# The response of the second half through the columns of U, in stacked bands

## What is computed

```python
U_o = gram_schmidt(U); V_o = gram_schmidt(V)        # 256 x 32 each
basis = U_o @ V_o.T
pooled = hidden.mean(axis=1)
h1 = relu(pooled @ gate_w1.T + gate_b1)
base_act = sigmoid(h1 @ gate_w2.T + gate_b2)
strength = base_act * sigmoid(score)
feats = (hidden @ basis) @ basis.T[:, :32]
response = feats @ resp_w.T + resp_b + safety_bias
out = hidden + strength * response
```

## Time and profile before

| | us |
|---|---|
| median of 3 runs | 1368.19 |
| lowest and highest | 1367.77, 1368.98 |
| profiled execution, its own time | 1369.96 |
| span of the profiled execution | 1367.8 |
| first half, about | 0 to 880 |
| turn between the halves, about | 880 to 905 |
| second half, about | 905 to 1368 |

### The profile page before, as it was taken

The page is one execution under the profiler, slowest core; times in us unless marked ns, Lnnn a source line. Parts: engine busy times, 40 slices in busy tenths (PEclk is TensorE's granted clock), DMA queues, the critical chain, the costliest instruction groups (busy, mean ns, idle before and its releaser), DMA issues. The chain is left out here.

```text
span 1367.8 us, 39618 instructions
## 1 busy us (share of the span) xinstructions
PE 1321.2 (97%) x11936; PEld 1119.3 (82%) x11936; DVE 1075.3 (79%) x3638; ACT 1071.8 (78%) x2664; POOL 871.5 (64%) x874
## 2 busy tenths in 40 slices
PE   4999999999999999999999998789999999999997
PEld 3777777777777777777777776579999999999997
DVE  4777777787877777778778777578888888888885
ACT  1788888888888888888888886777777777777773
POOL 4999989989999998998999998311222222122210
PEclk9999999999999999999999999989999999999998
DMA  9546656555564665655556482101010110111100
GB/s 289 184 152 200 191 161 207 166 188 181 169 210 152 197 191 159 208 164 187 181 169 210 154 259 70 32 24 40 31 46 31 35 42 31 46 31 41 36 24 32
DMA packets 182670, 175.07 MB, mean 128 GB/s; under 512 B 15552, under 2 KB 182112, under 8 KB 182624
## 3 DMA queue, kind: packets, MB, share of 16 engines
q1 hardware_dynamic: 181248, 173.64, 40.1%
q10 hardware_dynamic: 1376, 0.85, 0.2%
HBM read 157.69 MB, written 16.78 MB: 128 GB/s over the span
## 5 line engine op out<-in xcount | busy, mean ns | idle before, releaser
L428 POOL TENSOR_TENSOR ring<-ring,maskv 128x1024 f32<-128x1024 f32 x256 | 600.0, 2373 | 12.4 <-DMA ring<-in_fside 5.1
L912 ACT ACTIVATE ring<-ring,nmax 128x256 f32<-128x256 f32 x1024 | 452.5, 501 | 24.6 <-DVE nmax L606 24.6
L606 DVE CUSTOM_DVE_ANT_0 ring<-bank,ring 128x256 f32<-128x256 f32 x1024 | 373.0, 418 | 90.4 <-PE bank L1176 73.5
L917 ACT ACTIVATE pT<-bank 128x512 f32<-128x512 f32 x416 | 239.5, 592 | 103.5 <-PE bank L1191 103.4
L1191 PE MATMUL bank<-ident,ring 128*128 128x128 f32 x2048 | 292.6, 278 | 1.4 <-ACT pT L917 1.1
L1191 PEld LDWEIGHTS bank<-ident,ring 128*128 128x128 f32 x2048 | 231.9, 143 | 70.6 <-issue 47.9
L1047 ACT ACTIVATE work<-bank,b1t 128x256 f32<-128x256 f32 x256 | 107.6, 476 | 109.0 <-PE bank L1390 109.0
L1176 PE MATMUL bank<-work 32*128 32x256 f32 x2048 | 148.4, 404 | 6.0 <-DVE nmax L606 5.2
L1390 PE MATMUL bank<-hT_high,w_high 128*128 128x256 f32 x512 | 147.9, 289 | 3.4 <-DVE hT_rest L781 3.4
L1403 PE MATMUL bank<-w_high,gT_high 128*128 128x256 f32 x512 | 148.1, 289 | 0.0
L1403 PE MATMUL bank<-w_rest,gT_high 128*128 128x256 f32 x512 | 145.3, 284 | 0.0
(11 more groups left out here) (162 smaller groups left out, 2730.5 us busy)
## 6 DMA issues: line engine op xcount, KB each, us to landing
ring<-in_fside SPq DMA_DIRECT2D x128, 1024.0 KB, 7.7
xt<-in_x SPq DMA_DIRECT2D x32, 256.0 KB, 3.2
x_d<-x2s SPq DMA_DIRECT2D x32, 256.0 KB, 7.8
work<-x_d SPq DMA_DIRECT2D x32, 256.0 KB, 2.8
out<-pT SPq DMA_DIRECT2D x32, 256.0 KB, 2.2
mk<-in_mask SPq DMA_DIRECT2D x32, 64.0 KB, 6.7
w<-in_W SPq DMA_DIRECT2D x2, 1024.0 KB, 10.5
wada<-in_W_ada SPq DMA_DIRECT2D x1, 512.0 KB, 8.1
```

What stands on the lines that cost most here:

```text
L428: nc.gpsimd.tensor_tensor(v, v, m, ALU.add).then_inc(s_masked, 1)
L606: nc.vector.tensor_tensor_reduce(out=v, in0=score_ps[h % HG][:, qt], in1=v, scale=-1.0, scalar=ROW_MAX_NEG, op0=ALU.add, op1=ALU.min, accu ...
L912: nc.scalar.activation(v, v, ACT.Exp, bias=nmax[:, b.par, h, qt:qt + 1], scale=-1.0).then_inc(s_exp, 1)
L917: nc.scalar.activation(pT[:, h % (2 * HG)], tp_ps[h % 2], ACT.Copy).then_inc(s_pta, 1)
```

## The change

- M is no longer built. `response_matrix` keeps step 0 without the transposes of U_o, and step 1, whose stationary operand is gram repeated four times along its columns. So T comes out four times, stacked in four bands of 32 partitions, in bank 5 (`t_ps`). DVE copies only gram (with the repetition) and t1.
- ACT copies U_o to fp32r with its 32 columns repeated four times (`us[0]`), and T to `ts`; DVE makes the rest part of U_o (`us[1]`) and subtracts in bands 1 and 3 of `ts`, so that these hold the rest of T and bands 0 and 2 the high part.
- In the loop `response` is split. `reduce_z` makes z = U_o^T hidden^T, four times stacked (128 x 256), with 2 x 3 matmuls, in the second half of bank 6. ACT's new `z_high` copies it to `zs`, DVE's new `z_rest` replaces bands 2 and 3 by the rest part. The new `response` is one matmul for each 128 rows, whose 128 contracted rows hold high x high, high x rest, rest x high and rest x rest: 2 matmuls.
- Order. PE: `reduce_z` stands where `response` stood, `response` after the second `down`. ACT: `z_high` after `hT_out`. DVE: `hidT_rest` moves from behind `gT_rest(3)` to the very start of the step, `gate_hidden` from ahead of `gate_sum` to behind `gT_rest(3)`, `z_rest` stands behind `gate_sum`, `rsp_out` moves from there to behind `strength`.
- Waits: `hidT_rest` and `hidT_out` wait for the last `reduce_z` (semaphore `s2_zp`) in place of the last `response`; `reduce_z` also waits for `gate_hidden` of its batch; `hid_transpose` and the next `reduce_z` wait for `z_rest`; PE no longer waits for the copy of M ahead of the second half.

The diff, with declarations of semaphores left out:

```diff
@@ -139,7 +139,7 @@
         nrm = sb("nrm", [P, 2]); nrme = sb("nrme", [P, 2]); rnrm = sb("rnrm", [P, 2]); qcol = sb("qcol", [P, 2, DC]); gprod = sb("gprod", [P, 2, DC, R]); coef = sb("coef", [P, 2, R])
-        respT = sb("respT", [R, D]); gram = sb("gram", [R, R]); t1 = sb("t1", [R, D]); t2 = sb("t2", [R, D]); uoT = sb("uoT", [R, D]); resp_m = sb("resp_m", [P, DC, D])
+        respT = sb("respT", [R, D]); gram = sb("gram", [R, HG, R]); t1 = sb("t1", [R, D])
@@ -171,7 +171,8 @@
         hidTs = [lay("hidT_high", [P, DC, S], xt_at), lay("hidT_rest", [P, DC, S], xt_at + 4 * DC * S)]
-        resp_ms = [lay("resp_m_high", [P, DC, D], xres_at), lay("resp_m_rest", [P, DC, D], xres_at + 4 * DC * D)]
+        us = [lay("u_high", [P, DC, P], xres_at), lay("u_rest", [P, DC, P], xres_at + 4 * DC * P)]
+        ts, zs = lay("t_parts", [P, D], xres_at + 4 * 2 * DC * P), lay("z_parts", [P, S], xres_at + 4 * (2 * DC * P + D))
         regions = [work[:], pT[:].rearrange("p h t s -> p (h t s)")]
@@ -208,6 +209,7 @@
         prep_ps = tiles2(7)
+        z_ps, t_ps = bank[6][:, S:2 * S], bank[5][:, 0:D]
         gs_ps = bank[7][:, 0:2 * R].rearrange("p (a r) -> p a r", a=2)
@@ -580,18 +582,11 @@
-            def response_matrix(step):
-
-                dve.wait_ge(s_rm, step + 1)
-                if step == 0:
-                    nc.vector.tensor_copy(gram[:], bank[0][0:R, 0:R])
-                    nc.vector.tensor_copy(t1[:], bank[1][0:R, 0:D])
-                    nc.vector.tensor_copy(uoT[:], bank[2][0:R, 0:D]).then_inc(s_rmc, 1)
-                if step == 1:
-                    nc.vector.tensor_copy(t2[:], bank[3][0:R, 0:D]).then_inc(s_rmc, 1)
-                if step == 2:
-                    nc.vector.tensor_copy(resp_m[:], tiles2(1)).then_inc(s_rmc, 1)
-
+            def response_matrix():
+
+                dve.wait_ge(s_rm, 1)
+                nc.vector.tensor_copy(gram[:], bank[0][0:R, 0:R].unsqueeze(1).to_broadcast([R, HG, R]))
+                nc.vector.tensor_copy(t1[:], bank[1][0:R, 0:D]).then_inc(s_rmc, 1)
@@ -760,10 +755,8 @@
                 if n == B:
-                    response_matrix(0)
+                    response_matrix()
                     split_weights(0)
-                    response_matrix(1)
-                    response_matrix(2)
@@ -834,8 +827,13 @@
                 if b.i is not None or b.off >= 1:
-                    dve.wait_ge(s2_r, b.n)
+                    dve.wait_ge(s2_zp, b.n)
                 nc.vector.tensor_tensor(hidTs[1], hidT, f32(hidTs[0]), ALU.subtract).then_inc(s2_hidl, 1)
+
+            def z_rest(b):
+
+                dve.wait_ge(s2_zh, b.n + 1)
+                nc.vector.tensor_tensor(zs[2 * R:4 * R], z_ps[2 * R:4 * R], f32(zs[2 * R:4 * R]), ALU.subtract).then_inc(s2_zl, 1)
@@ -854,18 +852,25 @@
             dve.wait_ge(s2_m, 1)
-            nc.vector.tensor_tensor(resp_ms[1], resp_m[:], f32(resp_ms[0]), ALU.subtract).then_inc(s2_ml, 1)
+            nc.vector.tensor_tensor(us[1].rearrange("p c (k r) -> p c k r", k=HG), uv[:, 0].unsqueeze(2).to_broadcast([P, DC, HG, R]),
+                                    f32(us[0]).rearrange("p c (k r) -> p c k r", k=HG), ALU.subtract)
+            for k in (1, 3):
+                rows = slice(R * k, R * (k + 1))
+                ins = nc.vector.tensor_tensor(ts[rows], t_ps[rows], f32(ts[rows]), ALU.subtract)
+            ins.then_inc(s2_ml, 1)
...
                 tail2 = n is None or n >= 2
+                if tail2:
+                    hidT_rest(b.plus(-2))
                 if main:
...
                 if tail2:
-                    hidT_rest(b.plus(-2))
+                    gate_hidden(b.plus(-2))
                 if n is None or n + 2 < B:
@@ -874,9 +879,8 @@
                 if tail2:
-                    gate_hidden(b.plus(-2))
                     gate_sum(b.plus(-2))
-                    rsp_out(b.plus(-2))
+                    z_rest(b.plus(-2))
                 if main:
@@ -884,6 +888,7 @@
                     strength(b.plus(-2))
+                    rsp_out(b.plus(-2))
                     fin_out(b.plus(-2))
@@ -1063,7 +1068,7 @@
                 if b.i is not None or b.off >= 1:
-                    act.wait_ge(s2_r, b.n)
+                    act.wait_ge(s2_zp, b.n)
                     act.wait_ge(s2_h1p, b.n)
@@ -1072,6 +1077,12 @@
+            def z_high(b):
+                act.wait_ge(s2_zp, b.n + 1)
+                if b.i is not None or b.off >= 1:
+                    act.wait_ge(s2_r, b.n)
+                nc.scalar.activation(zs, z_ps, ACT.Copy).then_inc(s2_zh, 1)
+
             def gate2(b):
@@ -1081,9 +1092,10 @@
-            act.wait_ge(s_rmc, 3)
+            act.wait_ge(s_rm, 2)
             act.wait_ge(s_x2, B)
-            nc.scalar.activation(resp_ms[0], resp_m[:], ACT.Copy).then_inc(s2_m, 1)
+            nc.scalar.activation(us[0].rearrange("p c (k r) -> p c k r", k=HG), uv[:, 0].unsqueeze(2).to_broadcast([P, DC, HG, R]), ACT.Copy)
+            nc.scalar.activation(ts, t_ps, ACT.Copy).then_inc(s2_m, 1)
             yn_out(Batch(1))
@@ -1100,6 +1112,9 @@
                         hT_out(b.plus(1))
+                if tail2:
+                    z_high(b.plus(-2))
+                if main:
                     tanh_pair(b, 2)
@@ -1151,16 +1166,10 @@
                         mm(bank[0][0:R, 0:R], uv[:, 1, c], uv[:, 1, c], start=(c == 0), stop=(c == DC - 1))
-                    mm(bank[1][0:R, 0:D], uv[0:R, 0, 0], respT[:], start=True, stop=True)
-                    for c in range(DC):
-                        ins = nc.tensor.transpose(bank[2][0:R, c * P:(c + 1) * P], uv[:, 0, c], ident[:])
+                    ins = mm(bank[1][0:R, 0:D], uv[0:R, 0, 0], respT[:], start=True, stop=True)
                 if step == 1:
                     pe.wait_ge(s_rmc, 1)
-                    ins = mm(bank[3][0:R, 0:D], gram[:], t1[:], start=True, stop=True)
-                if step == 2:
-                    pe.wait_ge(s_rmc, 2)
-                    for c in range(DC):
-                        ins = mm(bank[1][:, c * D:(c + 1) * D], uoT[:, c * P:(c + 1) * P], t2[:], start=True, stop=True)
+                    ins = mm(t_ps, gram[:].rearrange("p k r -> p (k r)"), t1[:], start=True, stop=True)
                 ins.then_inc(s_rm, 1)
@@ -1362,16 +1371,11 @@
                     pv(b, 2)
-                if n == B:
-                    response_matrix(2)
-
             run_batches(pe, 0, 3, B - 3, B + 1, body)
...
             pe.wait_ge(s_x2, B)
-            pe.wait_ge(s_rmc, 3)
-
             def up_pair(b, j):
@@ -1409,6 +1413,7 @@
                     pe.wait_ge(s2_h1, b.n)
+                    pe.wait_ge(s2_zl, b.n)
                 for c in range(DC):
@@ -1420,17 +1425,24 @@
-            def response(b):
+            def reduce_z(b):
                 pe.wait_ge(s2_hidl, b.n + 1)
-                if b.i is not None or b.off >= 1:
-                    pe.wait_ge(s2_rs, b.n)
+                pe.wait_ge(s2_h1, b.n + 1)
+                if b.i is not None or b.off >= 1:
+                    pe.wait_ge(s2_zl, b.n)
                 else:
                     pe.wait_ge(s2_ml, 1)
+                for c in range(DC):
+                    for k, (kw, kx) in enumerate(HI_LO):
+                        ins = mm(z_ps, us[kw][:, c], hidTs[kx][:, c], start=(c == 0 and k == 0), stop=(c == DC - 1 and k == len(HI_LO) - 1))
+                ins.then_inc(s2_zp, 1)
+
+            def response(b):
+                pe.wait_ge(s2_zl, b.n + 1)
+                if b.i is not None or b.off >= 1:
+                    pe.wait_ge(s2_rs, b.n)
                 for t in range(QT):
-                    for c in range(DC):
-                        for k, (kx, kw) in enumerate(HI_LO):
-                            ins = mm(tiles2(5)[:, t], hidTs[kx][:, c, t * P:(t + 1) * P], resp_ms[kw][:, c],
-                                     start=(c == 0 and k == 0), stop=(c == DC - 1 and k == len(HI_LO) - 1))
+                    ins = mm(tiles2(5)[:, t], zs[:, t * P:(t + 1) * P], ts, start=True, stop=True)
                 ins.then_inc(s2_r, 1)
@@ -1447,11 +1459,13 @@
                 if tail2:
+                    reduce_z(b.plus(-2))
+                if main:
+                    up_pair(b, 2)
+                if tail:
+                    down(b.plus(-1), 1)
+                if tail2:
                     response(b.plus(-2))
-                if main:
-                    up_pair(b, 2)
-                if tail:
-                    down(b.plus(-1), 1)
                 if main:
```

(26 more changed lines are left out.)

## The result

The changed kernel takes 1352.7 us (median of 4 runs, 1352.31 to 1353.10), the kernel before 1368.1 (1367.77 to 1368.98). The ratio is 0.9882, 95% interval 0.9869 to 0.9895: 15.4 us or 1.1% faster (the rounded medians are 1368.09 and 1352.70). The forecast was 1351.8 us, in a range from 1349.5 to 1358. The profiled execution took 1352.78 us, its span is 1350.6.

A forecast was written before the change was run, and what follows sets the result against it. PE was taken to bound the second half's loop. From the median of 1368.19 us, -14.2 (loop), -0.7 (response 30), -1.9 (turn) and +0.4 (end) sum to -16.4, forecasting 1351.8 us, range 1349.5 to 1358.

The forecast's parts named there:

- The bound and the step: Second-half loop: PE is the bound; four matmuls fewer at 0.118 us save 0.47 us a step, 14.15 to 13.68.
- The slacks: Loop: added work is hidden, with 0.5 us idle ahead of the third `gate_pair` and 1.4 us for the round trip.
- DVE has room: Loop: DVE would be busy for 12.1 to 12.5 of 13.68 us a step, 89 to 92%.
- Rival B: Loop: waits eat part of the gain, 0.1 to 0.4 us a step, 1355 to 1364 us; chance 0.13.
- The order by itself: DVE's new order in the loop: worth nothing by itself, only makes room for `z_rest`.
- one microsecond ahead: Loop: `gate_hidden`, which `reduce_z` waits for, runs at 1111.4, one microsecond ahead of PE's 1112.43.
- The turn: Between the halves: `hT_rest` of batch 0 and PE start 1.9 us earlier; bounds 0 and 2.2.
- rival C: Loop: DVE-POOL collisions on moved operations twice a step make DVE the bound, slower than before, 1380 us; chance 0.03.
- Rival A: Turn gives back less because the PE clock's return may not follow the restart: 1352.6 us, other cases 1353.7 or 1351; chance 0.15.
- The end: Last step, all latency: the longer chain costs net +0.4 us, between 0 and 1.2.
- The sum: Whole kernel: -14.2 - 0.7 - 1.9 + 0.4 = -16.4 us, giving 1351.8 us from the median.

The follow-up runs named there:

- Experiments 1 and 2: First: changed kernel with four matmuls more in each `reduce_z`, 1368.3 us. Second: kernel before with four matmuls less in each `response`, 1355.0 us.
- experiments 5 and 6: Changed kernel with two, then four, idle additions on DVE in each step ahead of the third `gate_pair`: 1356.3 us and 1391.0 us.
- experiment 2: Kernel before with 8 matmuls in place of 12 in `response`, nothing else changed: 1355.0 us.
- experiment 4, a_gate_old: Changed kernel with `gate_hidden` back at its old place on DVE, ahead of `gate_sum`: 1483.7 us.
- b_8mm: Kernel before with the rest x high pass left out of `response`, 8 matmuls in place of 12: 1355.0 us.
- b_hoist: Kernel before with `add_b2` of batch 1 moved ahead of `inv_std2` of batch 2 on POOL: 1368.8 us.
- a_turn2: Changed kernel with two idle additions on DVE (1.2 us) right ahead of `hT_rest` of batch 0: 1352.6 us.
- a_again: The changed kernel itself, run once more beside other versions on one chip: 1352.3 us.
- a_pad4: Changed kernel with four idle additions on DVE in each step, ahead of the third `gate_pair`: 1391.0 us.
- a_hid_old: Changed kernel with `hidT_rest` back at its old place on DVE, behind `gT_rest(3)`: 1353.9 us.
- a_12mm: Changed kernel with four matmuls more in each `reduce_z`, ahead of its six and overwritten by them: 1368.3 us.
- a_pad2: Changed kernel with two idle additions on DVE in each step, ahead of the third `gate_pair`: 1356.3 us.
- a_hoist: Changed kernel with `add_b2` of batch 1 moved ahead of `inv_std2` of batch 2 on POOL: 1350.9 us.
- a_hoist2: Changed kernel with the same POOL move as a_hoist, repeated beside the changed kernel on the same chip: 1352.0 us.
- a_hoist_turn2: Changed kernel with `add_b2` of batch 1 moved ahead on POOL and two idle DVE additions ahead of `hT_rest` of batch 0: 1353.1 us.

## Why the prediction was right, point by point

- **The bound and the step.** PE stayed the bound, and a matmul costs its distance. 0.473 us a step were forecast, 0.498 came out, of which 0.48 is seen at the response itself (1.42 to 0.94). The other 0.02 lies in the two stretches of 24 matmuls ahead of `y_transpose` and behind `gate_h1`, each about 0.01 us shorter; why stays open. Experiments 1 and 2 tie 0.47 of it to the count of matmuls.
- **The slacks.** 0.5 us ahead of the third `gate_pair` was forecast (0.65 measured), 1.4 us for the round trip (1.5 measured), `z_rest` 0.4 us (0.43), `fin_out` about 1.2 (1.00), `rsp_out` free beside POOL (0.68 against 0.69 before). The sentence that DVE has room was right. Its size was rough, and these experiments answer a question that the prediction left at "room": a full DVE keeps holes of half a microsecond a step (experiments 5 and 6). Rival B didn't come: there is no wait of PE in the loop.
- **The order by itself** was called worth nothing. That holds for `hidT_rest`. For `gate_hidden` "it only makes room for `z_rest`" is too little: the old order is as good with the old waits (experiment 2), but `reduce_z` now waits for `gate_hidden`, and with that wait its old place costs 131 us (experiment 4). The forecast wasn't hurt, since the prediction had checked this wait at the new place, "one microsecond ahead".
- **The turn**: forecast -1.9, measured -1.1 here and -0.6 to -0.8 in the five other executions. The term was mis-sized by what it left out. The start itself came 2.0 us earlier in most executions, as forecast, and 2.6 in this one. But I followed the gain only to PE's start and not to the next wait, `hT_rest` of batch 1, whose collision with `add_b2` stood in the earlier trace rows and went into rival C alone. Rival A had the right kind of loss (the clock) at the wrong place: the return did move, from 22.2 to 17.1 us behind the cut (by the granted clock), and the clock fell a second time. Where the clock falls and returns differs between executions: of the first 24 matmuls of the second half all ran slow in four executions (the kernel before, `b_8mm`, `b_hoist`, `a_turn2`) and 14 to 16 in the ten others, and in eight of these the first 3 to 10 still ran at full clock. The Trainium skill, page "TensorE: Matmul & The Clock Gate", section "What's actually happening", says that the gate's window runs free of the kernel's start. By that, executions of the same instructions should scatter, and the traces bear it out only in part: of nine executions with the same list on PE and DVE up to there, three (the changed kernel, `a_again`, `a_pad4`) are back at full clock 0.7 to 1.5 us ahead of the others, but those six agree to 0.1 us, and so do the three of the old turn.
- **The end**: forecast +0.4, between 0 and 1.2; measured +1.2, and +0.6 in `a_hid_old`. The mis-sized term is the matmuls: I took the six at nearly full clock, and they ran at half of it, from a first one of 0.55 us on; the two of the last `response` took 0.80 us where I had allowed some 0.6.
- **The sum**: -14.9 for the steps against -15.5, -1.9 against -1.1, +0.4 against +1.2: errors of -0.6, +0.8 and +0.8 us, in sum 1.0 us, and so 1351.8 against 1352.7. The loop and its mechanism were forecast; that the total is off by one microsecond only is in part luck, for the error of the loop has the other sign than those of the turn and the end. The profiled execution of before was 1.8 us above its median, and 1.7 us of the difference of the two traces lie in the first half; to carry the sum over to the median, and not to subtract it from the span, was right.

## What to carry to other kernels

When one engine is busy for a whole loop, count its instructions times their distance from start to start, and spend the argument on whether the additions elsewhere fit in: look for each added wait at who must be done first and at what stands ahead of it in its engine's list. A gain at a place where engines start up one behind the other must be followed to the second and third wait, not only to the first: here an earlier start ran into a longer wait, and behind the longer wait the clock fell as well. Idle time of an engine is an upper bound of what it can take on; about two thirds of it (1.15 of 1.67 us a step) could be used here.

## What the runs showed of the hardware that I had not expected

- At PE's second wait of the turn, 2.4 us were followed by a stretch at the half clock in all seven executions that had such a wait (the changed kernel, `a_again`, `a_12mm`, `a_hid_old`, `a_gate_old`, `a_pad2`, `a_pad4`); 1.2 to 1.4 us at the same place were not, in six (the kernel before, `b_8mm`, `a_turn2`, `a_hoist`, `a_hoist2`, `a_hoist_turn2`). The length of the last wait alone isn't the rule, though: behind the first wait of the turn, of 1.7 to 1.9 us, a slow stretch followed in all nine executions that had it, in eight of them only after 3 to 10 matmuls at full clock (in `a_hoist` nine, from 896.35 on). Ahead of that wait stood another of 3.1 to 3.2 us, so what PE did further back may count too; no run tests it. Waits of 2.6 to 3.0 us in each step of `a_gate_old` brought the mean clock of the loop down to 0.90.
- From `hid_out` of batch 28 to the end, seven executions of kernels that have the same instructions there (the changed kernel, `a_again`, `a_hoist`, `a_hoist2`, `a_turn2`, `a_hoist_turn2` and, with `hidT_rest` elsewhere, `a_hid_old`) took 48.7 to 50.8 us. In `a_hid_old` it is 48.68 against 50.74 in the changed kernel; in this window its clock stayed at 1.00 where the other's fell:

```profile
1329.00:1336.00 7.00, 5.26 (x45) 5.02 (x44) 5.94 (x13) 3.23 (x9) 0.00 (x0) 1.00 0.11 37
```

```profile
1329.00:1336.00 7.00, 5.49 (x34) 5.50 (x35) 3.84 (x10) 2.61 (x8) 0.00 (x0) 0.76 0.11 37
```

- The first half scatters by 5.4 us between executions of the same code. A trace of one execution can't be subtracted from another as a whole. Between two cuts of the same kind it can: to 0.01 us in the loop, but only to about 0.6 us at the turn and 2 us at the end, where the clock falls at different moments.
